# Edge stage of a graph kernel: both inner layers in the step's own turn, the last layer one step and the sums two steps behind, in place of lags of one to four

## The reference

```python
fs = _mlp(x_send, flux_...); fr = _mlp(x_recv, flux_...)          # per edge
flux_send = einsum('ecd,ed->ec', fs.reshape(n_e, c, 2), nvec)     # flux_recv likewise
a_ws = _mlp((x_send + x_recv) * 0.5, a_Wh, a_bh, a_Wo, a_bo, a_ln_w, a_ln_b)
flux = 0.5 * (flux_send + flux_recv) - 0.5 * a_ws * (x_send - x_recv)
return x + segment_sum(flux, dst)
...
x = _layernorm(x + L0(x)); x = _layernorm(x + L1(x))
```

## Time and profile before

| | us |
|---|---|
| median of 3 runs (lowest, highest) | 7591.77 (7582.73, 7594.1) |
| profiled execution, its own time | 7593.69 |
| its span, first to last instruction | 7589.4 |
| PE busy | 5859.6 (77%) |
| DVE busy | 3564.4 (47%) |
| ACT busy | 2894.7 (38%) |
| POOL busy | 5391.2 (71%) |

### The profile page before, as it was taken

How to read it: one execution, slowest core, us unless ns; L and a number is a source line. 1 busy time by engine, 2 the same in 40 slices (tenths; PEclk the granted TensorE clock), 3 DMA queues, 4 the chain that set the end, 5 groups by cost and what they waited for, 6 DMA issues and landing times. The chain is left out here.

```text
span 7589.4 us, 219950 instructions
## 1 busy us (share of the span) xinstructions
PE 5859.6 (77%) x80654; PEld 4900.6 (65%) x80654; DVE 3564.4 (47%) x7629; ACT 2894.7 (38%) x5496; POOL 5391.2 (71%) x5204
## 2 busy tenths in 40 slices
PE   0159999999999999967777777777777777777775
PEld 0149999999999999955555555555555555555554
DVE  5459999872222344433344443444443444444443
ACT  0158888870000111113343434343434344434333
POOL 5777767647776766637777777777777777777774
PEclk9999999999999999978888888888888888888887
DMA  5233433437666666635555555555555555555553
GB/s 121 74 117 133 149 132 135 147 129 253 225 226 218 206 208 202 210 117 133 139 145 143 143 142 145 142 142 146 144 142 144 143 142 146 142 143 143 145 141 95
DMA packets 650540, 1155.65 MB, mean 152 GB/s; under 512 B 398567, under 2 KB 457127, under 8 KB 632148
## 3 DMA queue, kind: packets, MB, share of 16 engines
q0 software_dynamic: 217440, 521.49, 27.9%
q1 hardware_dynamic: 416862, 589.94, 23.9%
q10 hardware_dynamic: 15142, 28.94, 1.3%
HBM read 931.93 MB, written 207.96 MB: 150 GB/s over the span
## 5 line engine op out<-in xcount | busy, mean ns | idle before, releaser
L1700 POOL DMA_INDIRECT edge_rows<-node_table,edge_et x3224 | 3149.9, 977 | 988.2 <-issue 945.5
L809 POOL DMA_INDIRECT two_rows<-x_parts,src_at x1120 | 1092.9, 976 | 560.1 <-issue 354.7
L1227 PE MATMUL two_acc<-x_parts,two_win 128*128 128x192 bf16 x16072 | 1396.3, 248 | 36.8 <-issue 20.0
L1227 PEld LDWEIGHTS two_acc<-x_parts,two_win 128*128 128x128 fp8e4 x16072 | 1351.9, 99 | 50.4 <-issue 38.6
L989 ACT ACTIVATE one_win<-one_count 128x784 fp8e4<-128x784 f32 x1312 | 1072.9, 824 | 137.0 <-PE one_count L950 64.8
L1894 DVE TENSOR_TENSOR edge_zx<-edge_zp,edge_rows 128x512 f32<-128x512 f32 x403 | 279.0, 692 | 1758.8 <-ACT edge_z L1799 1674.6
L1728 PE MATMUL edge_mp<-edge_h,edge_W 128*128 128x512 f32 x1612 | 1098.7, 819 | 0.0
L1786 ACT ACTIVATE edge_yc<-edge_rows 128x512 f32<-128x512 f32 x403 | 254.0, 630 | 2182.5 <-DMA edge_rows<-node_table,edge_et 2182.5
L809 POOL DMA_INDIRECT one_rows<-x_parts,src_at x560 | 832.9, 1487 | 336.0 <-PE one_edge_acc L1013 172.5
L1760 PE MATMUL edge_seg<-edge_seg,edge_edge_now 128*1 128x66 f32 x6448 | 294.6, 229 | 836.7 <-ACT edge_seg L1815 833.0
L936 PE MATMUL one_acc<-x_parts,one_win 128*128 128x192 bf16 x8036 | 859.3, 246 | 0.5 <-ACT one_win L989 0.5
(11 more groups left out here) (319 smaller groups left out, 10831.8 us busy)
## 6 DMA issues: line engine op xcount, KB each, us to landing
two_win<-adjacency SPq DMA_DIRECT2D x82, 3136.0 KB
adjacency<-one_win SPq DMA_DIRECT2D x41, 3136.0 KB
edge_near<-near_ids SPq DMA_DIRECT2D x403, 192.0 KB
edge_rows<-node_table,edge_et POOLq DMA_INDIRECT x3224
node_sums<-edge_seg SPq DMA_DIRECT2D x806, 33.0 KB
two_rows<-x_parts,src_at POOLq DMA_INDIRECT x1120
edge_yd<-y_parts SPq DMA_DIRECT2D x806, 12.0 KB
node_table<-two_row SPq DMA_DIRECT2D x49, 260.0 KB
```

The lines of the kernel that those rows point to most:

```text
L809: pool.indirect_dma_start(rows[:, b % 2, e, :], None, XP.rearrange("p (j c) -> (p j) c", c=3 * C), bass.IndirectOffsetOnAxis(ap=src_at[:, ...
L1227: mm = pe.matmul(acc[b][:, half * 3 * C:(half + 1) * 3 * C], win[:, b, half, j, :].bitcast(FP8), now[:, j, :], start=(j == 0), stop=(j == ...
L1700: pool.indirect_dma_start(rows[:, h.b, t, :], None, T5, bass.IndirectOffsetOnAxis(ap=et[:, h.b, 0, t:t + 1].bitcast(I32), axis=0))\
```

## The change

The lists of stages are put in another order with other lags, the loops behind the last chunk are shortened to match, and VectorE's `LAG` goes from 5 to 2. `turn` and `take_y` move into the lists. No operation, buffer or wait is added or taken away; the waits have the same conditions in terms of chunks. SyncE's and GpSimd's code is unchanged.

```diff
-    LAG = 5
+    LAG = 2
...
             def step(h):
-                turn(h)
                 for k, run in stages:
                     if not early(h, k):
                         run(h.back(k))
 
-            stages = ((1, lambda h: layer(h, 1)), (2, lambda h: layer(h, 2)), (3, last), (4, sums))
+            stages = ((0, turn), (2, sums), (0, lambda h: layer(h, 1)), (1, last), (0, lambda h: layer(h, 2)))
             chunks(pe, step, HS, RB)
-            for c in range(HS, HS + 4):
+            for c in range(HS, HS + 2):
...
             def step(h):
-                take_y(h)
                 for k, run in stages:
...
-            stages = ((1, lambda h: relu(h, 0)), (2, lambda h: relu(h, 1)), (3, lambda h: relu(h, 2)), (4, squares), (5, take), (4, root))
+            stages = ((0, take_y), (0, lambda h: relu(h, 0)), (2, take), (0, lambda h: relu(h, 1)), (1, squares), (0, lambda h: relu(h, 2)), (1, root))
             chunks(act, step, HS, RB, DONE_LAG)
-            for c in range(HS, HS + 5):
+            for c in range(HS, HS + 2):
```

## The result

The changed kernel takes 8010.72 us (median of 4 runs, 8006.74 to 8020.04) against 7592.94: ratio 1.0549, 95% interval 1.0536 to 1.0563. It is slower by 418 us. The forecast was 7803, slower by 211, with a range to 7880. The direction was right, the size half of what came.

The account below looks back on a forecast made before the run. GpSimd's gathers were taken as the bound, SyncE only 3% faster. 45 rounds x (4.4 + 0.3) = 211 us, plus 5, less 5, gave 7805, or 7803 against the median; 8-in-10 range 7710 to 7880.

Parts of the forecast that it names:

- The serial step: ScalarE and TensorE: z 7.54 us after the copy of y, a step 9.9 us, under the gathers' 10.27; costs nothing.
- Late `out`: SyncE's store of finished rows: issued 11.3 us after the copy of y, in place of 6.04.
- The new wait: ScalarE's copy of the sums waits for a store to free its `seg` slot: 11 us with `out` late.
- They go at SyncE's pace: ScalarE's steps after the stall follow SyncE's stores; the loop makes a round 86.5 us, 4.4 more.
- Rival A: Only `out` is late, delaying `et`; copies do not wait for stores: 4.1 us a round, 185, 7777 us; chance 0.15.
- the second path: Late `out` delays `et`, then the gathers and the next `out`: a round of 85.5 us, 1.0 under the loop.
- Both ends: Start and tail of the edge stage: first `out` 5 us late, the last stores 4.7 us shorter.
- B: Gathers stay the bound, SyncE's lead swallows both waits, only the tail counts: 7587 us; chance 0.07.
- C: GpSimd's gathers get faster if `spread` falls between them: up to 87 us, forecast 7543 us; chance 0.05.
- D: TensorE at its lower clock most of the edge stage, rounds 6.2 us longer: 280 us, 7873 us; chance 0.12.

Follow-up runs that it names:

- r_early: Changed kernel with the root and last part of the finished nodes one turn earlier, whole sums: 7586.32 us, ratio 0.9985 to the kernel before.
- n_after: Changed kernel with the sums of a half in 5 products of 66 columns, three of four tiles left out: 7738.61 us, ratio 1.0193.
- r_ring: Changed kernel with the ring of the sums doubled to 16 halves, `out` still late: 7780.86 us, ratio 1.0241.
- g_before: Kernel before, unchanged, profiled at a time when it takes 11396 us: 11404 us.
- e_early: Changed kernel with root and last part of finished nodes one turn earlier, run when the kernel before took about 11400 us: 11799.76 us, ratio 1.0364.
- c_after: Changed kernel with the sums of a half in 5 products of 264 columns in place of 20 of 66: 7947.96 us, ratio 1.0462.

## Why the prediction was wrong, point by point

- **The serial step** (part 1). z was to come 7.54 after the copy of y and a step to take 9.9. In the step from 5595.13 z comes 7.76 after it, and steps without a wait take 10.0. Right for one step. But eight of them were then taken as 8 x 9.9 = 79.2 us, and r_early's eight take 82.1. That it costs nothing by itself was right by a hair: the gathers take the same 82.1.
- **Late `out`** (part 2). Forecast 11.3 behind the copy of y; 5545.16 - 5533.51 = 11.65. Right.
- **The new wait** (part 3). Place and cause right: one step of eight, the copies, for stores held back by `out`. A store was to be seen after 2.84; 2.89. The second copy was to come 13.9 behind `out` (5534.2 + 11 against 5525.97 + 5.3), and came 13.1 behind. The wait itself was to be 11 us; the rows have 5.35 + 5.98 of idle time, but some 2.5 of that ScalarE idles before these copies in any step. The second copy comes 14.45 into its step in place of 5.73, so 8.7 is the stall; that 11.3 is so near to 11 is luck.
- **"They go at SyncE's pace"** (part 3): this is the step that failed. The prediction let ScalarE, once freed, follow SyncE's 9.6 us a step to the next `out`, and closed the loop at 86.5. Its own sum gave a step of 9.9, longer than 9.6: after a stall ScalarE cannot follow SyncE, only fall further behind it. What the runs showed: a round is one stall and then serial steps to the next `out`, 91.63 us, with SyncE waiting 12.8 there. From the prediction's own numbers the round would have been: the late copy 13.9 behind `out`, 3.3 to the end of that step (copy, relu, z, root), six steps of 9.9, and 11.3 to the next `out`: 87.9, and 45 x 5.8 = 261 us. I compared the serial step with the gathers' 10.27 and never with the loop in which it now stood. n_after shows the missing comparison: shorten the step, and the predicted loop appears (85.46).
- **What was left out**, most of the 3.7 us between 87.9 and 91.6: the six steps behind the stall were 59.4 in this sum and took 62.6. 2.5 of these 3.2 stand in r_early as well, whose same six steps take 61.9: TensorE's late start (1.2 us of it), the longer products behind it, and steps a little over 9.9. Only the first step behind the stall is longer for it, 11.3 in place of 10.4, with a granted clock of 0.73 in place of 0.84. That the clock makes this 1.0 us is read from the rows; no run took it away. Nor did a run show why TensorE begins late. The sums now stand early in the step, where the clock is often still at its lower level: a product of L1751 took 287 ns in place of 222, while those of the layers fell from 819 to 683.
- **Rival A and the second path** (part 4). Late `out` through `et` alone was put by A at 4.1 us a round, so 86.2 and 185 us in all; r_ring has 86.10 and 185. Right, if TensorE's late start has no part in it. Part 4 had the same path at 85.5, with the waits of the copies beside it. In the changed kernel it plays no part: GpSimd waits for `et`, but ScalarE for rows in four places only.
- **Both ends**: small, as forecast. The first `out` comes 6 us late (forecast 5), the stretch behind the last is 7.9 us shorter (forecast 4.7); the rounds alone give 428, and the two profiled executions differ by 426.
- **Rivals B and C**: B was refuted by GpSimd's 500 us of waits for `et` and `seg_made` and by rounds of 91.6. C had the right sign and no weight: the mean gather fell from 977 to 968 ns, 3149.9 to 3120.2 us in all.
- **The upper end** of the range, D, took one mechanism (the lower clock) and not the sum of serial step and stall, so 7880 was too low.

## What to carry to other kernels

When a change shortens lags, list what each queue waits for once in a round, not only in a step: here a wait on the eighth step of another engine's queue became late by one long step and came back through a ring of buffers. A stall can be made up only if the serial steps are shorter than every other pace in the loop; compare them with each, and where they are not, add the stall in full to a round of serial steps. Take that round as a whole from a trace: a step summed from the rows of one step misses what happens once in eight. Before a new order is blamed, look for the one producer that it made late: moving that by a turn gave back all 418 us.

## What the runs showed of the hardware

The same kernel took 7596 and 11400 us at different times, once on the same chip. At 11400 the rounds of g_before were (11314.6 - 5394.1)/45 = 131.6 us, and 410 and 518 us of idle time stood on "issue" ahead of two kinds of weight loads of the sums. Times taken at such a moment can be compared only with each other, and their verdict (e_early still 3.6% slower) need not hold elsewhere (r_early 0.15% faster).

TensorE's queue can lose time at one fixed place of a loop of eight steps: its first product in the step two behind the one of the stall starts 2.05 us (after) and 2.20 us (r_early) behind the copy of y in place of 0.7 to 0.9, with nothing shown that it waits for. With 5 products for a half of the sums in place of 20 (c_after, n_after), with the doubled ring or with the sums three steps behind, it starts on time. The cause is open.

Narrow products feel the clock too. In the changed kernel, after 3.74 us of idle time before 5575.66, TensorE's granted clock was 0.50 from 5577.4 to 5579.0, its lower level, and the 128x66 products took 0.32 us; from 5579.2 to 5580.4 it was 0.99, and they took 0.22 to 0.24. A store of 33 KB from on-chip memory to `node_sums` was seen by the waiting ScalarE 2.39 and 2.89 us after its issue in the changed kernel, 2.84 in the kernel before.
